# Spreading the attention denominators: eight small matmuls in place of two wide ones in a one-core graph transformer layer

## The reference

```
Q = elu(x @ Wq) + 1 ;  K = elu(x @ Wk) + 1 ;  v = (x @ Wv) / L
KV = einsum('nshd,nshv->nhdv', K, v)
Z  = 1 / (einsum('nlhd,nhd->nlh', Q, K.sum(axis=1)) + ATT_EPS)     # one number per node and head
msg = einsum('nlhd,nhdv,nlh->nlhv', Q, KV, Z) * L
msg = layernorm(msg @ Wm, g1, b1) ; h = relu(concat([x, msg]) @ W1) @ W2 ; out = x + layernorm(h, g2, b2)
```

## Time and profile before

| what | value |
|---|---|
| median of three executions | 1430.46 us |
| the profiled execution, its time | 1430.72 us |
| its span | 1429.0 us |
| phase 1 with the stretch behind it | 0 to 274 us |
| phase 2 | 274 us to the end |
| first and last matmul pair of line 641 | 277.9 us, 1333.1 us |
| step length in the middle of phase 2 (line 641 to line 641, 712.7 to 757.4 in the trace) | about 44.3 us |

### The profile page before, as it was taken

How to read it: one execution, slowest core, us unless ns; L and a number is a source line. 1 busy time by engine, 2 the same in 40 slices (tenths; PEclk the granted TensorE clock), 3 DMA queues, 4 the chain that set the end, 5 groups by cost and what they waited for, 6 DMA issues and landing times.

```text
span 1429.0 us, 26739 instructions
## 1 busy us (share of the span) xinstructions
PE 1372.4 (96%) x8882; PEld 1233.0 (86%) x8882; DVE 1079.2 (76%) x2635; ACT 764.7 (54%) x1339; POOL 955.3 (67%) x873
## 2 busy tenths in 40 slices
PE   5999999778999999999999999999999999999987
PEld 4999999667888888888888888898888888888875
DVE  6776768657887787877878778787777877788761
ACT  3555555225555655555565456654565555655553
POOL 4767676477667776667766677666776667776352
PEclk9999999899999999999999999999999999999998
DMA  5787767222111221112221222212122121220000
GB/s 166 248 275 243 218 230 240 64 70 59 39 58 52 73 73 51 44 56 67 73 65 30 65 58 73 69 26 68 56 73 69 26 68 55 73 72 22 15 15 15
DMA packets 71630, 121.81 MB, mean 85 GB/s; under 512 B 38053, under 2 KB 42786, under 8 KB 71598
## 3 DMA queue, kind: packets, MB, share of 16 engines
q1 hardware_dynamic: 55598, 108.00, 23.8%
q0 software_dynamic: 16000, 13.43, 4.3%
HBM read 69.47 MB, written 51.70 MB: 85 GB/s over the span
## 4 chain that ended last, share of the span: by engine, by line
PE 91%; DVE 3%; POOL 2%; issue 1%; ACT 1%; DVEq 1%; POOLq 1%; DMA 0%; SPq 0%; ACTq 0%
PE psum L224 27%; PE psum L225 27%; PE psum L226 26%; PE psum L421 4%; PE psum L494 1%; PE psum L572 1%; PE psum L573 1%; PE psum L687 1%; PE psum L566 1%; PE psum L625 1%; PE psum L661 1%; PE psum L641 1%; POOL xg L1347 1%; POOL ag L1349 1%; DMA attn_bc<-in_L_gnn_attn_l 0%
## 5 line engine op out<-in xcount | busy, mean ns | idle before, releaser
L224 PE MATMUL psum<-w_hi,h_hi 128*125 128x256 f32 x600 | 171.8, 286 | 4.6 <-DVE h_lo L1233 3.7
L225 PE MATMUL psum<-w_lo,h_hi 128*125 128x256 f32 x600 | 170.0, 283 | 0.0
L226 PE MATMUL psum<-w_hi,h_lo 128*125 128x256 f32 x600 | 169.6, 283 | 0.0
L1347 POOL DMA_INDIRECT xg<-table_xt,idx x100 | 124.8, 1248 | 54.6 <-issue 54.6
L1353 POOL TENSOR_TENSOR h_lo<-relu,h_hi 128x1000 fp32r<-128x1000 f32 x50 | 127.4, 2568 | 29.8 <-ACT h_hi L789 29.8
L1153 DVE SCALAR_TENSOR_TENSOR base<-xb,rn,b_bc 125x256 f32<-125x256 f32 x100 | 144.6, 1486 | 0.3
L1349 POOL DMA_INDIRECT ag<-table_al,idx x100 | 121.0, 1210 | 30.4 <-issue 30.4
L1353 POOL TENSOR_TENSOR s_lo<-relu,s_hi 128x1000 fp32r<-128x1000 f32 (+1 forms) x50 | 90.6, 1812 | 71.4 <-ACT s_hi L789 71.4
L1353 POOL TENSOR_TENSOR e_lo<-relu,e_hi 128x1000 fp32r<-128x1000 f32 x50 | 115.9, 2342 | 16.5 <-DVE scale_rows L1122 16.2
L224 PE MATMUL psum<-xT_hi,w_hi 128*128 128x500 f32 x300 | 121.0, 403 | 1.3 <-ACT h_hi L789 1.3
L224 PE MATMUL psum<-z_hi,w_hi 128*128 128x500 f32 x300 | 119.4, 398 | 2.3 <-DVE z_lo L1184 2.3
(11 more groups left out here) (234 smaller groups left out, 4629.3 us busy)
## 6 DMA issues: line engine op xcount, KB each, us to landing
xb<-in_x SPq DMA_DIRECT2D x50, 448.0 KB
xT_hi_table<-x1T_hi SPq DMA_DIRECT2D x25, 500.0 KB
xT_lo_table<-x1T_lo SPq DMA_DIRECT2D x25, 500.0 KB
xT_hi<-xT_hi_table SPq DMA_DIRECT2D x25, 500.0 KB, 4.0
xT_lo<-xT_lo_table SPq DMA_DIRECT2D x25, 500.0 KB, 4.8
table_xt<-xts SPq DMA_DIRECT2D x25, 455.0 KB
out<-xmid SPq DMA_DIRECT2D x25, 448.0 KB
xb<-in_x SPq DMA_DIRECT2D x50, 52.0 KB
```

The costliest lines, as they stand in the source:

```text
L224: pe.matmul(out, wh, xh, start=first, stop=False)
L225: pe.matmul(out, wh, xl, start=False, stop=False)
L226: return pe.matmul(out, wl, xh, start=False, stop=last)
L1347: pool.indirect_dma_start(xg[par][:, j, :], None, table_xt.ap(), bass.IndirectOffsetOnAxis(idx[par][:, 1, j:j + 1], 0)).then_inc(S[f"gath{ ...
```

## The change

`rdenT` shrinks from 128 x 500 (block diagonal) to 128 x 126: the four tiles' rows stay where they stand on the partitions, all in the same columns 0 to 124, and one column more that stays zero. VectorE writes it with one instruction over 128 partitions in place of four over 32. What picked the tile by its columns is now picked by the weights: `den_sel` holds a matrix for each chunk q and each tile j, in which only tile j's 32 rows are not zero, so line 641 becomes eight matmuls of 126 columns, each with its own 128 x 128 weights, in place of two of 500. Tile j's result stands at columns 128j of the bank, no longer 125j, and the multiplication on VectorE reads it through a strided view. `dx` is still signalled once for each chunk, by the last of its four matmuls. The selection matrices are built by eight VectorE instructions in place of two, now straight from the identity.

```diff
-        low_rows = sb("low_rows", [P, QUAD + 1])
-        den_sel = sb("den_sel", [P, CK, P], F32R)
-        rdenT = sb("rdenT", [P, GR], F32R)
+        low_rows = sb("low_rows", [P, T + 1])
+        den_sel = sb("den_sel", [P, CK, T, P], F32R)
+        rdenT = sb("rdenT", [P, R + 1], F32R)
...
                     for q in range(CK):
-                        pe.matmul(colT(6 + q), den_sel[:, q, :], rdenT[:], start=True, stop=True).then_inc(S["dx"], 1)
+                        for j in range(T):
+                            last = pe.matmul(psum[:, 6 + q, j * P:j * P + R + 1], den_sel[:, q, j, :], rdenT[:],
+                                             start=True, stop=True)
+                        last.then_inc(S["dx"], 1)
...
-            dve.reduce_sum(low_rows[:, 0:QUAD], ident[:].rearrange("p (j r) -> p r j", r=QUAD), AXX)
+            for q in range(CK):
+                for j in range(T):
+                    rows = [QUAD * j + d + q * per for d in (0, MIX_HEADS)]
+                    tt(den_sel[:, q, j, :].rearrange("p (h n) -> p h n", h=per),
+                       ident[:, rows[0]:rows[0] + per].unsqueeze(2).broadcast_to([P, per, MIX_CH]),
+                       ident[:, rows[1]:rows[1] + per].unsqueeze(2).broadcast_to([P, per, MIX_CH]), ALU.add)
+            dve.reduce_sum(low_rows[:, 0:T], ident[:].rearrange("p (j r) -> p j r", r=QUAD)[:, :, MIX_HEADS:2 * MIX_HEADS],
+                           AXX)
             dve.drain()
-            for q in range(CK):
-                at = [d + q * per for d in (0, MIX_HEADS)]
-                tt(den_sel[:, q, :].rearrange("p (h n) -> p h n", h=per),
-                   low_rows[:, at[0]:at[0] + per].unsqueeze(2).broadcast_to([P, per, MIX_CH]),
-                   low_rows[:, at[1]:at[1] + per].unsqueeze(2).broadcast_to([P, per, MIX_CH]), ALU.add)
...
-                for j in range(T):
-                    part = slice(j * QUAD, (j + 1) * QUAD)
-                    last = stt(rdenT[part, j * R:(j + 1) * R], rden_hi[part, 0:R], low_rows[part, QUAD:QUAD + 1],
-                               rden[part, :], ALU.mult, ALU.add)
-                last.then_inc(S["den_rows"], 1)
+                stt(rdenT[:, 0:R], rden_hi[:, 0:R], low_rows[:, T:T + 1], rden, ALU.mult,
+                    ALU.add).then_inc(S["den_rows"], 1)
...
-                        tt(qf[:, q, :], qf[:, q, :], colT(6 + q), ALU.mult).then_inc(S["q_den"], 1)
+                        rows = qf[:, q, :].rearrange("p (j n) -> p j n", j=T)
+                        tt(rows, rows, psum[:, 6 + q, :].rearrange("p (j n) -> p j n", j=T)[:, :, 0:R],
+                           ALU.mult).then_inc(S["q_den"], 1)
```

More of the change, by code:

```diff
@@ L1038, in _ @@
             dve.wait_ge(S["xo0"], 4 * dma16(NG - 1, 0))
-            dve.reduce_sum(low_rows[:, 0:QUAD], ident[:].rearrange("p (j r) -> p r j", r=QUAD), AXX)
-            dve.drain()
-            for q in range(CK):
-                at = [d + q * per for d in (0, MIX_HEADS)]
-                tt(den_sel[:, q, :].rearrange("p (h n) -> p h n", h=per),
-                   low_rows[:, at[0]:at[0] + per].unsqueeze(2).broadcast_to([P, per, MIX_CH]),
-                   low_rows[:, at[1]:at[1] + per].unsqueeze(2).broadcast_to([P, per, MIX_CH]), ALU.add)
-            dve.reduce_sum(low_rows[:, QUAD:QUAD + 1], low_rows[:, MIX_HEADS:2 * MIX_HEADS], AXX)
+            for q in range(CK):
[6 more added lines that the diff above has]
+                           AXX)
+            dve.drain()
+            dve.reduce_sum(low_rows[:, T:T + 1], low_rows[:, 0:T], AXX)
             dve.drain()
-            ts(low_rows[:, QUAD:QUAD + 1], low_rows[:, QUAD:QUAD + 1], -1.0, None, ALU.mult)
+            ts(low_rows[:, T:T + 1], low_rows[:, T:T + 1], -1.0, None, ALU.mult)
             dve.wait_ge(S["g_hi"], 1)
```

## The result

The changed kernel takes 1439.63 us (median of 6 runs, 1438.76 to 1440.14) against 1429.99 us of the kernel before (6 runs, 1428.88 to 1430.72): +9.6 us, ratio 1.0066, 95% interval 1.0054 to 1.0079. The forecast was 1441 us, +0.7%. The profiled execution took 1439.86 us with a span of 1438.1; that of the kernel before took 1430.72.

A forecast was written before the change was run, and what follows sets the result against it. TensorE was taken to bound full steps of phase 2. The profiled 1430.72 us + 9.8 for 23 full steps + 0.5 at entry gave 1441.0, forecast 1441 us (+0.7%); range 1438 to 1463, reaching into a slower matmul mode.

The forecast's parts named there:

- The bound: Full steps of phase 2: TensorE, busy 1000.00 of 1000 us, pays added work in full; VectorE's saving returns nothing.
- The step on TensorE: Line 641, full step: eight matmuls at 0.110 us replace two, 0.88 for 0.454, +0.43 us (bounds +0.40 to +0.50).
- the load's pace: Line 508, one-column matmuls with 128-wide weights: 0.106 us each, taken as the pace of a weight load.
- The 23 full steps: Steps 2 to 24 of phase 2: 23 x 0.43 = +9.8 us, bounds +9.2 and +11.5.
- VectorE: Writes of `rdenT`: one instruction for four, 1.06 us less a step, 26 us in all, worth nothing in time.
- a slack of under 0.2 us becomes 1.2: Line 641, full step: `rdenT` is ready 1.06 us earlier, but TensorE did not wait, so worth nothing.
- The entry: Entry to phase 2, once, with its first two steps: together +0.5 us, bounds -0.3 and +1.5.
- step 0: First step of phase 2: gathers +1.0 and `mv_m` +0.5 to 0.75 us later, not additive; taken as +0.9.
- step 1: Second step of phase 2: TensorE's waits for `rdenT` and `z_lo` give back only 0.4 of 1.4 us.
- The slow mode: Rival, chance 0.17: line 641's short fp32r matmuls take 0.21 us each, +1.23 a step, 1461 us.
- Hidden loads: Rival, chance 0.07 (hidden or partly): line 641's weight loads hide, 0.063 us a matmul, +0.05 a step, 1432 us.
- a fourth of 128 partitions and a whole of them: VectorE's `rdenT` write: one instruction over 128 partitions costs the same 0.35 us as one over 32 (bounds 0.29 to 0.36).

The follow-up runs named there:

- the first experiment: Kernel before with only TensorE's matmuls of line 641 changed to eight of 126 columns, VectorE keeping its four writes: 1439.15 us against 1429.50, ratio 1.0069.

## Why the prediction was right

- **The bound.** TensorE bounds full steps, and the exchange is priced on it alone: right, shown from both sides by the two halves of the change run apart (+9.7 and -1.5 us, the latter not from full steps).
- **The step on TensorE.** Forecast +0.43 us (0.110 a matmul, bounds 0.107 to 0.119); measured +0.426, though the distance was 0.113, by which the same sum gives 0.45. That the two agree to the hundredth is luck of some 0.02 us a step. From the first transpose to the first product with `sW2` it is 0.39 more in the mean of the 23 full steps, and 0.05 more from that to the next product (0.28 for 0.23 in the rows), 0.44 together; the rest of the step gives 0.015 back, and I don't know where.
- **A reading that was too low.** The prediction took the load's pace from line 508 as 0.106 us, a mean over 15 distances. The first of these is 0.03 and the other 14 are 0.111 or 0.112. So the trace of the kernel before already had the 0.111 to 0.113 that the fp32r matmuls then took: one column and 126 columns cost the same against 128-wide weights. The pace measured lay inside the bounds (0.107 to 0.119), which came from plain fp32 and from the next wider fp32r matmul.
- **The 23 full steps.** Forecast +9.8 us; the 22 intervals measured give +9.37, times 23/22 makes 9.8.
- **VectorE.** Forecast 1.06 us a step less and 26 us in all; measured 25.8. The forecast that a slack of under 0.2 us becomes 1.2 holds in odd steps (0.13 before, 1.19 after, from the end of the write to the start of the load). In even steps, which the one step of the earlier trace rows does not show, it was 0.54 before and 1.20 or 1.57 after. The sum doesn't change by it. How near the edge it was is shown by the run with three more instructions: another 0.77 us on this chain are paid in part in every step.
- **The entry.** Forecast +0.9 for step 0, seen in one pair of traces +0.71 (23.71 less 23.00), which the spread of 22.66 to 24.06 above doesn't tell from nothing. Its parts, counted from the first features, came as forecast but for one: the gathers 1.0 us later (forecast 1.0), the eight matmuls 1.74 us in place of 0.97 (1.7 and 0.96), GpSimd's take-up of `mv_m` 0.43 later (0.5 to 1.0), but line 642 began 0.44 earlier than line 641 had, where I allowed 0.3. For step 1 I allowed 0.4 back and there was nothing: from the `row_n` transposes of step 1 to those of step 2 it took 35.97 and 35.99 us. Together +0.5 forecast, +0.7 seen; the term is too small to be judged.
- **Where 10.3 and 9.6 differ.** The 9.6 is a difference of medians, and its interval reaches from 7.7 to 11.3 us, so the 0.7 between them needs no cause. The two profiled executions differ by 9.1: +9.8 for the full steps, +0.7 at entry, and -1.5 for the stretch up to the first features (266.89 against 268.39), before any changed instruction runs; that makes 9.0. This stretch differs by as much between runs of kernels that have it in common (266.05 to 268.52 in the experiments).
- **The slow mode** (0.17) did not occur: 8 records, not 16, a step, and 250 columns at 0.116. **Hidden loads** (0.07) did not either: 64 columns cost as much as 126. The Trainium skill's 81 ns for a matmul at 128 columns with its load, and its fast load for 128 columns of weights that are not FP32 ("TensorE: Matmul & The Clock Gate", the two sections named in the prediction), are not what this case's fp32r matmuls show: 0.111 to 0.113 us.
- **Wrong in a detail:** a fourth of 128 partitions and a whole of them cost VectorE the same 0.35 us, I said. That is the duration of the record; the distance to the next instruction is 0.26 (758.57 to 758.83), so the four of them, 1.44 us to the next instruction, cost more than four such instructions would, and the change gave VectorE 1.18 us a step and not 1.06. It lay off the path.

## What to carry to other kernels

Before cutting a wide matmul into narrow ones with weights of their own, compare the columns with the load: here, as an estimate from 0.111 us a load and 6 ns and 0.44 ns a column, fewer than some 240 columns against 128-wide weights pay for the load and not for the data, and two matmuls of 250 cost what one of 500 does while four of 126 cost twice that. An exchange of work between engines is priced by the waits of a full step, not by busy shares: here 26 us off an engine with 24% idle time were worth no more than 0.2 us in 22 full steps, though 0.77 us more on it in each step cost 12 us. What decides is the slack at the place where one engine waits for the other, and it was under 0.1 us in every second step. Small constants built between two phases are best built in a wait of the engine that builds them, where all engines stand behind it: here that brought the first gather 1.2 and 2.2 us forward in the traces, though the times alone don't tell it.

## What the runs showed of the hardware

- VectorE's four instructions over 32 partitions each took longer to make room for the next than those over 128. In the run with three more instructions three of 128 x 125 came 0.257 us apart, and the write to partitions 0 to 31 followed the third at 0.25; the three writes behind it, each starting at the next 32 partitions, came (1.41 - 0.34) / 3 = 0.36 apart. Each of these began 0.015 us after the record in front had ended, while those 0.26 apart began 0.09 before it had. The Trainium skill has this in "VectorE: DVE Perf Modes", section "Two Vector instructions with no wait between them": an instruction whose operands start in another group of 32 partitions than those of the one in front starts only when all earlier ones have finished. The trace agrees. No run has instructions over 32 partitions that all start in the same place, so what the width by itself does isn't shown.
- The wait of TensorE on another engine shows as 0.05 us from the end of the writer's record to the start of the load at the granted clock of 2.4 GHz, and as 0.12 in step 0, where the granted clock was 0.50 (1.2 GHz). A slack read from a trace is to be counted from there.
- fp32r showed no slower mode at 250, 126 or 64 columns: 0.116, 0.113 and 0.112 us with 128-wide weights, 0.062 for 126 columns with 64-wide ones.
- The same weights four times in a row (the first experiment) are loaded four times and cost what four different ones do: 0.111 against 0.113 us, 200 loads in 25 steps in both.
